# A recurrent attention kernel: ScalarE takes the masked queries and the later key copies from GpSimd, and TensorE multiplies zeros in the prologue

## The chip, the cores and the metric

The kernel runs on one core of a Trainium2 chip. Its time is the device time of that core in microseconds (us). The core has TensorE (PE in the profile), VectorE (DVE), ScalarE (ACT), GpSimd (POOL) and SyncE (SP, which only issues DMAs here). They run at the same time, each in its own program order, and meet at semaphores. A ScalarE function comes from a table; a change of function group (square root, SiLU, sigmoid) puts a table load ahead of the activation.

## The reference

The input x has 4 sequences of 256 tokens with 256 channels. It is normalised (xn), and two branches are joined: x + attention(xn) * silu(experts(xn)).

The attention has 32 heads of 8 channels and goes through each sequence in 16 minibatches of 16 tokens. For each (sequence, head) pair it keeps a weight W1 (8 by 8) and a bias b1, and updates them after every minibatch:

```
Z1 = xk @ W1 + b1
grad = ln_fused_l2_bwd(Z1, xv - xk, ln_w, ln_b)
Z1_bar = xq @ W1 - eta * tril(xq @ xk.T) @ grad + b1 - tril(eta) @ grad
W1 = W1 - (eta_last * xk).T @ grad
b1 = b1 - sum(eta_last * grad)
out = xq + ln(Z1_bar, ln_w, ln_b)
```

The rows are then normalised and multiplied by o_w. The expert branch routes each token to 2 of 8 experts (256 to 2 x 128 to 256).

## The kernel before

**Tiling.** The 1024 tokens lie in 8 tiles (groups) of 128 rows: group j holds 32 tokens of each of the 4 sequences, that is two minibatches of 16. The 128 (sequence, head) pairs are the partitions of the recurrence.

**VectorE** runs the recurrence, one minibatch after another, in `minibatch` (16 calls, n = 0 to 15). A call multiplies keys by token (`KT`) with W (line 821), reduces (832), forms six small products, writes the variances `sxx` (846), and then needs ScalarE's square root (`sv`, semaphore `rstd`) at line 853. It ends with the gradient product (880), its reduction (885) and the new W. Between these steps other work is put as fills. The first minibatch of group j also transposes the keys and targets of group j + 1 out of PSUM (`KP`, `QP`, semaphore `pair_done`); it waits for `kts` before it reads `KT` of its own group.

**GpSimd** has a list written out by hand. For each group j from 1 to 7: `pad_grads(j-1)` (line 374, two halves), four or five `hidden_product(i)` (lines 350 and 355: expert slot i's gate times share, times up), four `mask_scores(j, i)` (line 290), `bias_targets(j+1)` (329 copies the keys from by-channel `KP` to by-token `KT`, 331 adds a bias to the targets), and at the end of the group `masked_queries(j+1)` (339: four multiplications by a head mask, from `xqT` into `xqm`). `masked_queries(0)` and `(1)` stand in the prologue, ahead of `lower_tiles(2, NG)`.

**ScalarE** copies PSUM out (`scores_out`, line 565; `expert_slot`, gate 582 and up 583; `xn_out`, 528) and takes the square roots (`step_std`, 571 and 572). In group j from 2 on its order is: one expert slot, a table load for the square root (`preload_sqrt`, 591), `scores_out(j, 1)`, `step_std(2j+1)`, `scores_out(j, 2)`, slot, `scores_out(j, 3)`, slot, `scores_out(j, 4)`, `preload_sqrt`, `step_std(2j+2)`, and the rest of the group's slots, the first of which loads the SiLU table. `expert_slot(i)` for i = 10, 18, 26 first writes a pair's output (`output_rows`, 587, semaphore `g`).

**TensorE** follows the same plan: `expert_slot(i)` computes slot i's 24 products (1174; it waits until ScalarE has emptied slot i-2) and slot i-2's product with `down` (1187; it waits for GpSimd's `hT`, and where a pair of tiles begins, for `g`); `tile(j, i)` makes a quarter of the scores (1133; it waits for the previous quarter's copy and for `queries`, the masked queries); `group_end(j-1)` multiplies by the padded gradients (1215), `group_start(j)` by W (1201), `next_pair_rows` makes keys and targets for two groups later. The expert slots are spread over groups 1 to 7 as 3, 5, 5, 5, 5, 5, 4.

**The prologue** fills the first 57 us. TensorE first multiplies seven zero matrices (`pe_warm`, line 1074), then makes key rows, rates and target rows of tile 0, transposes tiles 1 to 3 (`xn_channels`, 1081) when ScalarE has normalised them (518), and waits for their copy `xn_out` (528) before the keys of tile 1 (1115). In ScalarE's order `xn_out` of tiles 1 to 3 stands behind `input_std(2, 4, 8)`, the square root that tiles 4 to 7 need (507, released by VectorE).

The new ScalarE steps sit in this loop:

```
for j in range(1, NG):            # ScalarE
    ...
    scores_out(j, 1); step_std(2 * j + 1)
    ...                           # keys_by_token(j + 1) comes here
    scores_out(j, 2)
    ...
    scores_out(j, 4); preload_sqrt(2 * j + 1); step_std(2 * j + 2)
    ...                           # masked_queries(j + 1) comes here
    for i in slots: expert_slot(i)
```

Of the kernel before, what the change touches and what calls it, by code (L numbers as in the profile page):

```python
# [22 lines left out]
P = 128  # L23
B, L, HS = 4, 256, 256
NH, HD, K = 32, 8, 16
NG = 8
# [23 lines left out]
def build(nc, x_bt_d, small_d, wkv_d, wq_d, wlrt_d, gup_d, down_d, wo_d, out_d):  # L50
# [3 lines left out]
    with ExitStack() as ctx:  # L54
# [228 lines left out]
        def _(pool):  # L283
# [41 lines left out]
            def bias_targets(j):  # L325

                pool.wait_ge(S_["pair_done"] if j else S_["pair0T"], j or 1)
                if j:
                    pool.tensor_copy(KT[:, j % 2, :, 0:HD], KP[:, j % 2, 0:HD, :].rearrange("p c t -> p t c")).then_inc(S_["kts"], 1)
                q = QP[:, j % 2, :, :]  # L330
                pool.tensor_tensor(q, q, gb[:, :].unsqueeze(1).broadcast_to([P, GT, HD]), ALU.add).then_inc(S_["targets"], 1)

            def masked_queries(j):

                pool.wait_ge(S_["qchc"], 2 + 2 * (j // 4))
                if j >= 2:
                    pool.wait_ge(S_["sc"], 4 * (j - 1))
                for h in range(4):
                    pool.tensor_scalar(xqm[:, j % 2, :, :, h, :], xqT[:, :, :, GT * j:GT * j + GT],
                                       cmask[:, h:h + 1], 0.0, ALU.mult, ALU.add).then_inc(S_["queries"], 1)  # L340
# [92 lines left out]
            masked_queries(0)  # L433
            masked_queries(1)
# [24 lines left out]
            for j in range(1, NG):  # L459
# [22 lines left out]
                if j + 1 < NG:  # L482
                    masked_queries(j + 1)
# [13 lines left out]
        def _(act):  # L497
# [69 lines left out]

            def step_std(n):
# [20 lines left out]
            def preload_sqrt(n):  # L589

                act.activation(warm[:, n:n + 1], eps[:, :], ACT.Sqrt)  # L591
# [40 lines left out]
            step_std(0)  # L632
            input_std(2, 4, 8)
            xn_out((2, 4), 2, 1, 4)
# [13 lines left out]
            preload_sqrt(1)  # L648
            step_std(2)
# [5 lines left out]
            query_rows(1)  # L655
            for i in range(2, 5):
                scores_out(0, i)
            step_std(3)
            slot = 0
            for j in range(1, NG):  # L660
# [7 lines left out]
                else:  # L668
# [5 lines left out]
                    if j == 6:  # L674
                        norm_z(0)
                    scores_out(j, 2)
# [10 lines left out]
                if j == 4:  # L687
                    scores_out(j, 4)
                for i in slots:
                    expert_slot(i)  # L690
            act.wait_ge(S_["small2"], 16)
# [377 lines left out]
        def _(pe):  # L1069
# [184 lines left out]

            pe.wait_ge(S_["xn0"], 1)
# [7 lines left out]
            rates(0, 1)  # L1263
            pe.wait_ge(S_["wt"], 1)
            target_rows(0, bank[5][:, 0:256]).then_inc(S_["pair0"], 1)
            xn_channels((2, 4), 1, 4)
            pe.wait_ge(S_["xnTc"], 3)
# [59 lines left out]
            def zero_products(count):  # L1327
                for _ in range(count):
                    pe.matmul(bank[1][:, 0:256], pe_warm[:, 0:P], pe_warm[:, :], start=True, stop=True)

# [62 lines left out]
```

## Time and profile before

| what | value |
|---|---|
| median of 3 runs | 233.45 us (232.33 to 238.2) |
| the profiled execution | 233.13 us |
| its span, first to last instruction | 231.2 us |
| TensorE busy | 194.6 us (84%) |
| VectorE busy | 198.5 us (86%) |
| ScalarE busy | 115.7 us (50%) |
| GpSimd busy | 154.4 us (67%) |
| mean granted TensorE clock | 0.938 |

1.93 us of the profiled execution lie outside its span. "Busy" counts the time in which an engine executes; the rest is idle or issue time. Times in the timelines count from the span's start. A matmul in float32 shows as two records. "Granted clock" is 1.0 at the full 2.4 GHz and 0.5 at 1.2 GHz; a value between them is a stretch that has both.

### The profile page before, as it was taken

Reading aid. Unit: us, or ns where it says so; the run is one execution under the profiler, and the core shown is the slowest. Engines: PE = TensorE matmul, PEld = TensorE weight load, DVE = VectorE, ACT = ScalarE, POOL = GpSimd, SP = SyncE. Lnnn points to the kernel's source line nnn. Section 1 sums busy time; section 2 is a strip of 40 time slices with the busy share of each in tenths; the row PEclk is TensorE's granted clock in tenths of the full one; section 3 lists DMA queues with packets and bytes.
Section 4 is the critical chain, followed back from the end, with each engine's and each line's share of the span. In section 5 each row is a group of like instructions: output and inputs, shape, how many; then the busy total and the mean of one; then the engine's idle time right before and its main releaser. Section 6 shows DMA issues by size and latency. Waiting matters only on the chain.

```text
span 231.2 us, 5305 instructions
## 1 busy us (share of the span) xinstructions
PE 194.6 (84%) x1893; PEld 154.4 (67%) x1893; DVE 198.5 (86%) x525; ACT 115.7 (50%) x235; POOL 154.4 (67%) x212
## 2 busy tenths in 40 slices
PE   8533999778789979889999985999799599998772
PEld 6313567256678768677968873879588488866551
DVE  2899999999995999999999999999999999206962
ACT  2462179553529063736555755157564556147230
POOL 2314539897779458597687649769999977464234
PEclk9975899979999979999999999799999799988998
DMA  5995200217613000374120044103000300400022
GB/s 166 374 405 169 75 4 0 71 37 157 204 12 91 3 0 10 91 119 65 27 73 3 0 100 135 48 10 91 0 3 10 93 3 0 145 40 0 3 91 91
DMA packets 26000, 17.44 MB, mean 75 GB/s; under 512 B 10552, under 2 KB 24312, under 8 KB 25464
## 3 DMA queue, kind: packets, MB, share of 16 engines
q1 hardware_dynamic: 25464, 16.25, 25.2%
q10 hardware_dynamic: 512, 0.87, 1.2%
q8 instruction: 15, 0.25, 0.4%
q14 instruction: 9, 0.07, 0.1%
HBM read 15.22 MB, written 1.87 MB: 74 GB/s over the span
## 4 chain that ended last, share of the span: by engine, by line
DVE 38%; PE 34%; ACT 8%; POOL 8%; issue 7%; DMA 2%; POOLq 0%; SPq 0%; DVEq 0%; ACTq 0%
PE bank L1174 9%; PE bank L1215 7%; PE bank L1187 5%; PE bank L1133 5%; DVE pr L821 4%; DVE bank L832 4%; DVE pr L880 4%; DVE dW L885 3%; PE bank L1201 3%; POOL hT L355 2%; POOL gw L350 2%; DMA small<-in_small 2%; POOL sgpad L374 2%; PE bank L1251 2%; PE bank L1109 1%
## 5 line engine op out<-in xcount | busy, mean ns | idle before, releaser
L1174 PE MATMUL bank<-xn_hi,gup_hi 128*128 128x256 f32 x128 | 41.0, 320 | 1.6 <-ACT up L583 1.6
L1187 PE MATMUL bank<-down,hT 128*128 128x256 f32 x128 | 34.4, 393 | 4.5 <-ACT G L587 2.5
L350 POOL TENSOR_TENSOR gw<-gate,share 128x256 f32<-128x256 f32 x32 | 23.4, 730 | 21.5 <-ACT gate L582 21.0
L1174 PE MATMUL bank<-xn_hi,gup_lo 128*128 128x256 f32 x128 | 36.9, 288 | 0.0
L1174 PE MATMUL bank<-xn_lo,gup_hi 128*128 128x256 f32 x128 | 36.9, 288 | 0.0
L290 POOL TENSOR_TENSOR A<-A,mask 128x256 f32<-128x256 f32 x32 | 23.5, 735 | 13.2 <-ACT A L565 13.2
L1174 PEld LDWEIGHTS bank<-xn_hi,gup_hi 128*128 128x128 f32 x128 | 25.1, 196 | 7.6 <-issue 4.2
L1187 PEld LDWEIGHTS bank<-down,hT 128*128 128x128 f32 x128 | 22.9, 198 | 7.1 <-issue 2.7
L565 ACT ACTIVATE A<-bank,one 128x256 f32<-128x256 f32 x32 | 15.0, 469 | 23.2 <-PE bank L1133 23.2
L1174 PEld LDWEIGHTS bank<-xn_hi,gup_lo 128*128 128x128 f32 x128 | 25.2, 197 | 0.2
L355 POOL TENSOR_TENSOR hT<-gw,up 128x256 f32<-128x256 f32 x32 | 23.4, 730 | 2.9 <-PE bank L1187 0.5
L1174 PEld LDWEIGHTS bank<-xn_lo,gup_hi 128*128 128x128 f32 x128 | 25.2, 197 | 0.0
L1215 PE MATMUL bank<-sgpad,A 128*32 128x32 f32 x512 | 20.3, 207 | 5.4 <-POOL sgpad L374 5.4
L582 ACT ACTIVATE gate<-bank 128x256 f32<-128x256 f32 x32 | 12.3, 384 | 25.0 <-PE bank L1174 20.5
L1215 PEld LDWEIGHTS bank<-sgpad,A 128*32 128x32 f32 x512 | 19.5, 124 | 7.7 <-issue 7.7
L1133 PE MATMUL bank<-xqm,xkT 32*32 32x128 f32 x512 | 20.5, 274 | 4.4 <-ACT A L565 2.7
L821 DVE TENSOR_TENSOR pr<-KT,bank 128x1152 f32<-128x1152 f32 x16 | 21.6, 1350 | 0.3
L832 DVE TENSOR_REDUCE bank<-pr 128x128 f32<-128x1152 f32 x16 | 21.4, 1337 | 0.2
L1133 PEld LDWEIGHTS bank<-xqm,xkT 32*32 32x32 f32 x512 | 11.9, 104 | 13.5 <-issue 9.6
L880 DVE TENSOR_TENSOR pr<-KP,bank 128x1152 f32<-128x1152 f32 x15 | 20.3, 1354 | 0.5
L591 ACT ACT_TABLE_LOAD x16 | 20.5, 1283 | 0.3
L885 DVE TENSOR_REDUCE dW<-pr 128x72 f32<-128x1152 f32 x15 | 20.2, 1350 | 0.5
(158 smaller groups left out, 436.7 us busy)
## 6 DMA issues: line engine op xcount, KB each, us to landing
wblk<-w_blocks SPq DMA_DIRECT2D x8, 512.0 KB, 4.0
share<-shares SPq DMA_DIRECT2D x8, 512.0 KB, 8.3
sgpad<-in_gup SPq DMA_DIRECT2D x1, 1024.0 KB, 9.6
G<-in_gup SPq DMA_DIRECT2D x1, 1024.0 KB, 11.7
down<-in_down SPq DMA_DIRECT2D x1, 1024.0 KB, 14.2
xkT<-in_x_bt SPq DMA_DIRECT2D x1, 1024.0 KB, 4.8
out<-G SPq DMA_DIRECT2D x4, 256.0 KB, 2.5
wkv<-in_wkv ACTq DMA_DIRECT2D x1, 512.0 KB, 4.2
```

The costliest lines, as they stand in the source:

```text
L290: pool.tensor_tensor(scores, scores, mask_bc, ALU.mult).then_inc(S_["masked"], 1)
L350: pool.tensor_tensor(gw[:, :], gate[:, i % 2, :], share[:, pair % 2, e, :], ALU.mult).then_inc(S_["gw"], 1)
L355: pool.tensor_tensor(hT[:, i % 2, :], gw[:, :], up[:, i % 2, :], ALU.mult).then_inc(S_["h"], 1)
L591: act.activation(warm[:, n:n + 1], eps[:, :], ACT.Sqrt)
L821: v.tensor_tensor(pr1[:, :].rearrange("p (t d c) -> p t d c", d=HD, t=K), kt.unsqueeze(2).broadcast_to([P, K, HD, C1]), W.rearrange("p (d ...
L832: v.tensor_reduce(x_ps, pr1[:, :].rearrange("p (a c) -> p a c", c=C1), AX.X, ALU.add).then_inc(chain, 1)
L880: v.tensor_tensor(pr2[:, :].rearrange("p (d c t) -> p d c t", c=C1, d=HD), kp.unsqueeze(1).broadcast_to([P, HD, C1, K]), sg.unsqueeze(2).b ...
L885: v.tensor_reduce(dW[:, :], pr2[:, :].rearrange("p (a t) -> p a t", t=K), AX.X, ALU.add).then_inc(S_["sg"], 1)
L1133: ins = pe.matmul(bk[32 * b:32 * b + 32, P * hf:P * hf + P], xkT[32 * q:32 * q + 32, hf, j, GT * b:GT * b + GT], xqm[32 * q:32 * q + 32, j ...
L1174: ins = pe.matmul(bank[4 + i % 2][:, 2 * P * g:2 * P * g + 2 * P], w[:, k, e, NI * g:NI * g + NI].bitcast(F32R), x[:, k, 2 * pair:2 * pair ...
L1187: ins = pe.matmul(bank[7][:, HS * r:HS * r + HS], hT[:, i % 2, P * r:P * r + P], down[:, e, :], start=(e == 0 and r == 0), stop=(e == NE - ...
L1215: ins = pe.matmul(bank[hf][rows_j, 4 * HD * r:4 * HD * r + 4 * HD], A[:, j % 2, q, c:c + GT], sgpad[:, j % 2, h, :, :].rearrange("p b d -> ...
```

## The change

Three edits.

1. `masked_queries` moves from GpSimd to ScalarE: four activations with the mask as per-partition scale in place of four GpSimd multiplications, for all 8 groups. `(0)` stands ahead of `step_std(2)`, `(1)` behind `query_rows(1)`, and `(j+1)` behind `step_std(2j+2)`, ahead of the group's remaining expert slots. The key copy of `bias_targets` stays on GpSimd for groups 1 and 2, and for groups 3 to 7 is a ScalarE copy (`keys_by_token`) behind `step_std(2j+1)` and ahead of `scores_out(j, 2)`.
2. In the prologue ScalarE's `xn_out((2, 4), 2, 1, 4)` goes ahead of `input_std(2, 4, 8)`.
3. TensorE gets 2, 7 and 1 zero products in three places of the prologue.

```diff
             def bias_targets(j):
                 pool.wait_ge(S_["pair_done"] if j else S_["pair0T"], j or 1)
-                if j:
+                if j in (1, 2):
                     pool.tensor_copy(KT[:, j % 2, :, 0:HD], KP[...].rearrange("p c t -> p t c")).then_inc(S_["kts"], 1)
-            def masked_queries(j):                      # GpSimd
-                pool.wait_ge(S_["qchc"], 2 + 2 * (j // 4))
-                if j >= 2:
-                    pool.wait_ge(S_["sc"], 4 * (j - 1))
-                for h in range(4):
-                    pool.tensor_scalar(xqm[:, j % 2, :, :, h, :], xqT[:, :, :, GT * j:GT * j + GT],
-                                       cmask[:, h:h + 1], 0.0, ALU.mult, ALU.add).then_inc(S_["queries"], 1)
...
-            masked_queries(0)
-            masked_queries(1)
             lower_tiles(2, NG)
...
-                if j + 1 < NG:
-                    masked_queries(j + 1)
...
+            def masked_queries(j):                      # ScalarE
+                act.wait_ge(S_["qchc"], 2 + 2 * (j // 4))
+                if j >= 2:
+                    act.wait_ge(S_["sc"], 4 * (j - 1))
+                for h in range(4):
+                    act.activation(xqm[:, j % 2, :, :, h, :], xqT[:, :, :, GT * j:GT * j + GT], ACT.Copy,
+                                   scale=cmask[:, h:h + 1]).then_inc(S_["queries"], 1)
+            def keys_by_token(j):
+                act.wait_ge(S_["pair_done"], j)
+                act.copy(KT[:, j % 2, :, 0:HD], KP[...].rearrange("p c t -> p t c")).then_inc(S_["kts"], 1)
...
             step_std(0)
+            xn_out((2, 4), 2, 1, 4)
             input_std(2, 4, 8)
-            xn_out((2, 4), 2, 1, 4)
...
             preload_sqrt(1)
+            act.wait_ge(S_["small2"], 16)
+            masked_queries(0)
             step_std(2)
...
             query_rows(1)
+            masked_queries(1)
             for i in range(2, 5):
                 scores_out(0, i)
...
+                    if j < NG - 1:
+                        keys_by_token(j + 1)
                     scores_out(j, 2)
...
+                if j < NG - 1:
+                    masked_queries(j + 1)
                 for i in slots:
                     expert_slot(i)
...
             rates(0, 1)                                 # TensorE
+            zero_products(2)
             pe.wait_ge(S_["wt"], 1)
             target_rows(0, bank[5][:, 0:256]).then_inc(S_["pair0"], 1)
+            zero_products(7)
             xn_channels((2, 4), 1, 4)
+            zero_products(1)
```

`zero_products(count)` multiplies `pe_warm` by itself into `bank[1]` count times, 128 by 128 by 256; the function only moves up in the source.

## Rows read from the trace of the kernel before

**Rows 1.** The page: chain of waits by engine, share of the span.

```profile
DVE 38%; PE 34%; ACT 8%; POOL 8%; issue 7%; DMA 2%; POOLq 0%; SPq 0%; DVEq 0%; ACTq 0%
```

**Rows 2.** Waits: who waited for whom: us in total, times, longest.

```profile
ACT sv L571 <- DVE sxx L846: 28.9, 12, 5.7
...
PE bank L1215 <- POOL sgpad L374: 5.4, 5, 1.7
```

**Rows 3.** Timeline of VectorE: start us, us, instruction, [idle before, releaser].

```profile
71.80 0.36 DVE L853 RECIPROCAL bank<-sv 128x32 f32<-128x32 f32 x1 [2.62 <-ACT sv L572]
```

**Rows 4.** Chain of waits, end of group 6: start us, us, what.

```profile
179.27 0.20 DVE sxx L846
...
179.71 0.29 ACT sv L572
...
180.02 0.84 ACT L587
...
181.31 0.60 ACT G L587
...
182.06 2.04 PE bank L1187 x4
```

**Rows 5.** Windows: engine busy us (instructions) in a stretch, TensorE clock, DMA.

```profile
15.30:17.50 2.20, 1.92 (x6) 1.08 (x6) 2.17 (x9) 1.29 (x4) 0.00 (x0) 0.50 1.14 413
...
182.00:186.00 4.00, 3.94 (x17) 3.62 (x17) 3.79 (x13) 0.46 (x2) 2.73 (x5) 0.57 0.14 36
186.00:202.00 16.00, 16.00 (x211) 13.71 (x210) 11.52 (x32) 7.96 (x19) 10.91 (x14) 1.00 0.16 45
```

**Rows 6.** GpSimd, line 339: count, duration ns min/median/max.

```profile
L339 POOL TENSOR_SCALAR xqm<-xqT,small x32: 472/478/483, 45.6 to 182.8; 128x256 f32<-128x256 f32 x32
```

**Rows 7.** GpSimd, line 329, the same view.

```profile
L329 POOL COPY KT<-KP x7: 617/625/650, 27.6 to 170.2; 128x256 f32<-128x256 f32 x7
```

**Rows 8.** Chain of waits, end of group 4.

```profile
137.06 1.22 POOL xqm L339 x3
```

**Rows 9.** ScalarE, line 518, durations.

```profile
L518 ACT ACTIVATE xn<-xn,rstd_in x3: 492/492/493, 14.8 to 15.6; 128x256 f32<-128x256 f32 x3
```

**Rows 10.** Timeline of ScalarE: two runs of activations, one after another.

```profile
14.80 1.29 ACT L518 ACTIVATE xn<-xn,rstd_in 128x256 f32<-128x256 f32 x3
...
220.59 1.51 ACT L622 ACTIVATE xqm<-bank,small 128x128 f32<-128x128 f32 x4 [0.70 <-PE bank L1241]
```

**Rows 11.** Timeline of ScalarE: idle time before some instructions.

```profile
19.79 0.30 ACT L507 ACTIVATE std_in<-mv,eps_in 128x4 f32<-128x4 f32 x1 [2.28 <-DVE mv L720]
...
47.09 0.31 ACT L571 ACTIVATE sv<-sxx,eps 128x16 f32<-128x16 f32 x1 [2.35 <-DVE sxx L846]
...
53.82 0.47 ACT L565 ACTIVATE A<-bank,one 128x256 f32<-128x256 f32 x1 [2.83 <-PE bank L1133]
...
124.22 0.31 ACT L571 ACTIVATE sv<-sxx,eps 128x16 f32<-128x16 f32 x1 [2.15 <-DVE sxx L846]
...
167.98 0.31 ACT L571 ACTIVATE sv<-sxx,eps 128x16 f32<-128x16 f32 x1 [1.01 <-DVE sxx L846]
...
179.50 0.31 ACT L571 ACTIVATE sv<-sxx,eps 128x16 f32<-128x16 f32 x1 [1.36 <-DVE sxx L846]
```

**Rows 12.** Timeline of TensorE: products and idle time before them.

```profile
10.13 1.13 PE L1109 MATMUL bank<-wt,xnT 128*128 128x256 f32 x4 [1.31 <-DVE wt L746]
15.35 1.92 PE L1081 MATMUL bank<-small,xn 128*128 128x128 f32 x6 [4.09 <-ACT xn L518]
...
42.06 3.70 PE L1088 MATMUL bank<-xnT,wq 128*128 128x512 f32 x8 [0.94 <-ACT xkT L535]
...
47.59 0.64 PE L1133 MATMUL bank<-xqm,xkT 32*32 32x128 f32 x16 [1.61 <-POOL xqm L339]
...
95.05 0.39 PE L1174 MATMUL bank<-xn_hi,gup_hi 128*128 128x256 f32 x1 [0.92 <-ACT up L583]
...
182.06 1.19 PE L1187 MATMUL bank<-down,hT 128*128 128x256 f32 x2 [2.48 <-ACT G L587]
```

More of the change, by code:

```diff
@@ L566, in scores_out @@
                                bias=one[:, 0:1]).then_inc(S_["scored"], 1)
+            def masked_queries(j):
[7 more added lines that the diff above has]
+                act.wait_ge(S_["pair_done"], j)
+                act.copy(KT[:, j % 2, :, 0:HD], KP[:, j % 2, 0:HD, :].rearrange("p c t -> p t c")).then_inc(S_["kts"], 1)
             def step_std(n):
@@ L688, in _ @@
                     scores_out(j, 4)
+                if j < NG - 1:
+                    masked_queries(j + 1)
                 for i in slots:
                     expert_slot(i)
-            act.wait_ge(S_["small2"], 16)
             preload_sqrt(0)
@@ L1253, in project, with zero_products @@
                 ins.then_inc(S_["o"], 1)
+            def zero_products(count):
+                for _ in range(count):
+                    pe.matmul(bank[1][:, 0:256], pe_warm[:, 0:P], pe_warm[:, :], start=True, stop=True)
             pe.wait_ge(S_["xn0"], 1)
@@ L1326, in _ @@
                 project(f)
-            def zero_products(count):
-                for _ in range(count):
-                    pe.matmul(bank[1][:, 0:256], pe_warm[:, 0:P], pe_warm[:, :], start=True, stop=True)
             pe.wait_ge(S_["zc"], 8)
```

## The prediction, made before the changed kernel was run

> **What bounds the kernel now.** I read the chain of waits on the page first: VectorE has 38% of it, TensorE 34%, ScalarE and GpSimd 8% each [rows 1]. So no engine bounds it alone, and GpSimd's share is small although it is busy for two thirds of the span. The list of waits says who is early: ScalarE waited 28.9 us in total, 12 times, for VectorE's variances [rows 2]. VectorE thus leads through the loop over groups. The reader should check the other direction, VectorE waiting for ScalarE: the one long such wait is 2.62 us at 71.80, in group 2 [rows 3]. Then comes the question where VectorE's lead passes to the end. The chain at the end of group 6 answers it: VectorE's variances at 179.27, ScalarE's square roots, a SiLU table load at 180.02, the copy of an output pair (line 587) at 181.31, and only then TensorE's product at 182.06 [rows 4], which had been waiting for 2.48 us [rows 12]. From there TensorE has no gap: in the 16 us from 186 to 202 it is busy for 16.00 at full clock [rows 5]. The end is therefore the variances of minibatch 14, plus what ScalarE does until it writes that output pair, plus a TensorE backlog that nothing shortens.
>
> **What leaves GpSimd.** 32 multiplications of 0.478 us [rows 6] and five copies of 0.625 us [rows 7]: about 15 + 3 = 18 us of its time. Is that time on the path? In the end stage GpSimd's masked queries (the last at 182.8 [rows 6]) stand beside TensorE's busy stretch, whose start ScalarE decides [rows 4]. One place has them on the chain, 1.22 us and a fourth instruction at 137.06, in group 4 [rows 8]. What is late next there is VectorE: ScalarE waits for it again by 167.98 (1.01 us) and 179.50 (1.36 us) [rows 11]. I take 0 us for the relief of GpSimd. Its two bounds: nothing, and a gain of the 5.4 us that TensorE spent waiting for GpSimd's padded gradients [rows 2].
>
> **What ScalarE gets.** No row shows a masked query on ScalarE. The nearest is the scaled copy of line 518: same size, same function, scale by a per-partition column, no table load before it. Three take 1.29 us and one lasts 0.492, so one follows another after (1.29 - 0.492) / 2 = 0.40 us [rows 9, 10]. Four cost 1.6 us. The ends: 0.35 us each (line 622, half the size, four in 1.51 us [rows 10]) gives 1.4; 0.492 each, without overlap, gives 2.0. A key copy costs the same 0.4 to 0.5 us.
>
> Place by place:
> - `masked_queries(0)`: ScalarE was idle for 2.35 us before `step_std(2)` at 47.09 [rows 11]; 1.6 us fit. TensorE's first scores, which waited 1.61 us for GpSimd at 47.59 [rows 12], start about 1 us sooner, but their copy stands behind that same `step_std(2)`: 0 us.
> - `masked_queries(1)`: ScalarE was idle for 2.83 us before the second scores copy at 53.82 [rows 11]; 0 us. Without that cover it would be 1.6 us on the path into group 1.
> - `keys_by_token`, five times: behind the square roots, so VectorE does not wait for it there; it delays one scores copy by about 0.45 us. VectorE needs `KT` only in the next group. 0 us, at most 5 x 0.45 = 2.3 us.
> - `masked_queries(2)` to `(6)`: they stand behind `step_std(2j+2)` and ahead of the table load and the gates of the group's last slots. Queued behind them are the gates, then GpSimd's products and padded gradients, then TensorE. At 95.05 TensorE already waited 0.92 us for such a gate [rows 12]; it will wait 1.6 us longer. VectorE does not feel this until ScalarE's next square root comes late, and there ScalarE had 2.15 us to spare at 124.22 [rows 11]: 1.6 us fit. In groups 4 and 5 GpSimd's own 4 x 0.478 = 1.9 us are gone from the same stretch, so ScalarE's 1.6 replace them. 0 us.
> - `masked_queries(7)`: between the square roots of 179.71 and the table load of 180.02 [rows 4]. No cover: TensorE is waiting for what comes behind it, and the backlog behind is solid. **+1.6 us**, whole, on the path. GpSimd's copy of this work, now gone, gives nothing back, since the hidden product after it needs the gate that ScalarE makes late.
>
> **The prologue.** `xn_out` sooner: the copy waited behind a square root that VectorE released at 19.79 [rows 11]; its input is there when the transposes end at 15.35 + 1.92 = 17.3 [rows 12], so the keys of tile 1 come some 2.5 us sooner. The stretch after the 4.09 us wait of TensorE ran at 0.50 of the clock, 1.2 GHz [rows 5, 12]; with zeros in the wait it should stay at 2.4 GHz, and the transposes and key rows are shorter. A zero product is a 128x256 product in float32; two take 1.13 us with their fill at full clock [rows 12], so at most 0.57 us each: two are 1.1 us in a wait of 1.31, seven are 4.0 us in one of 4.09 [rows 12]. If the clock is low they overrun the wait of 4.09 by about 3 us, which `xn_out` hides again, because before it started only after 19.79. What does the head start buy? TensorE next meets ScalarE's copies, which go by VectorE's order (high halves, sigmoid, square roots): at 42.06 it waited 0.94 us for one [rows 12], and now waits more than 2. VectorE has no room to gain in (2.17 us busy of 2.20 [rows 5]). 0 us; bounds -0.5 us (the group 1 chain starts a little warmer) and +1 us (the longer wait ahead of 42.06 costs clock).
>
> **The rule on ports.** The removed GpSimd instructions last 0.472 to 0.483 us and 0.617 to 0.650 us over the whole span [rows 6, 7], beside a VectorE that is nearly always busy: neither engine seems to block the other, and I take 0 us. The Trainium skill, page "SBUF — State Buffer", section "Who interferes with whom", says that VectorE and GpSimd share a port pair, that a VectorE instruction with two SBUF inputs and a GpSimd instruction that reads SBUF block each other, and that ScalarE never waits; by that the move would also make VectorE faster. That mechanism is one form of rival C.
>
> **The sum.** 1.6 us on the path. The profiled execution took 233.13 us, 1.93 us of it outside the span of 231.2; 233.13 + 1.6 = 234.7. The median of the three runs, 233.45, lies 0.3 us above that execution, less than the sum is sure to.
>
> **The rivals.**
> - **B, ScalarE's delay is paid more than once.** The longer waits of TensorE (0.92 + 1.6 = 2.5 us at 95.05) are like the 2.48 us before 182.06, behind which the clock was 0.57 for 4 us [rows 5, 12]: 4 x 0.43 = 1.7 us lost. Then TensorE is 3.3 us late in group 3, 1.2 more than the 2.15 to spare [rows 11], and VectorE stalls: 234.7 + 1.2 = 235.9. In the full form no slack is left and each of the groups 1 to 6 pays its 1.6 us: 233.1 + 9.6 = 242.7, **slower**. It decides from the point where ScalarE reaches a square root after VectorE's variances. For: the spare times of 1.01 and 1.36 us [rows 11] are under 1.6. Against: those two come where GpSimd's load falls away too.
> - **C, VectorE gets ahead.** GpSimd's instructions hold VectorE up unseen, or the stall of 2.62 us [rows 3] goes away. If one of the removed multiplications had blocked VectorE in each of the groups 1 to 6, it would be 6 x 0.48 = 2.9 us earlier: 234.7 - 2.9 = 231.8; the stall gives 234.7 - 2.6 = 232.1. Against: the even durations [rows 6, 7]; and the stall starts at a chain that VectorE's own third minibatch releases, through gates that the change leaves alone.
> - **D, GpSimd was the limit.** TensorE's 5.4 us of waiting for padded gradients [rows 2] go, and they counted: 233.1 - 5.4 = 227.7. Against: ScalarE kept waiting for VectorE [rows 2], so the time returns as that wait.
> - **E, it changes nothing.** Masked queries at the end of group 6 hidden: 233.1. It needs VectorE or the output copy to be earlier by 1.6 us, for which I see no row.
>
> **How the numbers follow.** My case (234.7, its own range 233.4 to 236) has 0.56; B in the small form 0.11 and in the full form 0.07; C 0.13; E 0.08; D 0.05. The range goes from 231.5 to 237.0: it takes in C, E, my case and small B, with 0.3 us either way for the runs, and leaves out D and full B. Two per cent of 233.45 is 4.7 us, about what a measurement of this kernel can tell from no change (its three runs spread over 5.9 us); 228.8 and 238.1 are the bounds. Faster is D: 0.05. Slower is full B: 0.07. The rest, 0.88, is the same.
>
> **What would show it.** TensorE's granted clock near 1.0 from 11 to 25 us, the key rows of tile 1 starting near 18.4, and yet VectorE's variances of minibatch 2 and of 14 at the same times as before (within 0.3 us). ScalarE: four copies in 1.6 us between lines 572 and the SiLU load, the output copy (587) at 182.9 in place of 181.31, and TensorE's product behind it at 183.7. GpSimd 18 us less busy. I am wrong if the variances of minibatch 14 move by more than 1 us (down: C or D; up: B), if TensorE's stretch behind 183.7 has gaps, or if four masked queries take much other than 1.6 us.

## The result and the profile after

The changed kernel took **241.07 us** (median of 4 runs, 237.81 to 242.2); the kernel before took 233.03 us in the same series (232.33 to 238.2). The ratio is 1.0246, with an interval of 1.0179 to 1.0312. A second series, run later as an experiment, gave 239.28 us and 1.0279 [1.0182, 1.0376]. The ratios leave out executions more than 1.5% above the fastest of their kernel, so they are smaller than the ratio of the two medians. The forecast was 234.7 us, with a range up to 237.0: too low. Both series say slower; whether the loss is above or below 2% they leave just open.

The profiled execution is one of the longer ones: 242.2 us, 9.1 us more than the profiled one of before. Its page:

```profile
span 240.4 us, 5346 instructions
...
PE 205.8 (86%) x1913; PEld 161.5 (67%) x1913; DVE 198.3 (82%) x525; ACT 131.0 (55%) x272; POOL 137.2 (57%) x175
...
DVE 52%; PE 28%; ACT 7%; issue 6%; DMA 3%; POOL 2%; POOLq 0%; DVEq 0%; SPq 0%; ACTq 0%
```

GpSimd is 17.2 us less busy, as planned, and ScalarE 15.3 us busier. The chain has shifted from TensorE and GpSimd to VectorE [rows 1]. I take VectorE's sixteen variances as milestones, because ScalarE's root, and through it everything else, hangs on them. `sxx(n)`, in us from the span's start:

| n | 0 | 4 | 5 | 9 | 10 | 14 | 15 | product at the end of group 6 | span |
|---|---|---|---|---|---|---|---|---|---|
| before | 16.69 | 68.44 | 81.01 | 123.91 | 135.09 | 179.19 | 190.91 | 182.06 | 231.2 |
| after | 17.86 | 69.56 | 86.17 | 129.02 | 141.01 | 184.97 | 196.69 | 189.43 | 240.4 |
| later by | 1.17 | 1.12 | 5.16 | 5.11 | 5.92 | 5.78 | 5.78 | 7.37 | 9.2 |

The reader sees five separate losses, and long stretches where nothing changes: 1.2 us before the first minibatch, 4.0 in minibatch 5, 0.8 in minibatch 10, 1.6 behind minibatch 14, and 1.8 in the tail.

**The start, 1.2 us.** VectorE's first work on the small inputs waits for a SyncE transfer. It began at 6.33 before. Timeline of VectorE after:

```profile
7.49 0.17 DVE L741 TENSOR_TENSOR g<-small 128x8 f32<-128x8 f32 x1 [2.04 <-DMA small<-in_small]
```

The same transfer, by the list of DMA issues in the first 9 us, took 4.9 us from issue to landing before and 6.1 us after:

```profile
small<-in_small SPq DMA_DIRECT2D x1, 252.5 KB, 4.9
```

```profile
small<-in_small SPq DMA_DIRECT2D x1, 252.5 KB, 6.1
```

**Minibatch 5, 4.0 us.** The reader should follow the chain of waits of the changed kernel from GpSimd's padded gradients to VectorE's reciprocal:

```profile
62.20 1.06 POOL sgpad L365
...
63.40 2.83 PE bank L1222 x64
66.24 1.05 PE bank L1140 x16
...
67.84 1.07 PE bank L1140 x16
68.91 2.86 PE bank L1181 x12
71.77 1.71 PE bank L1194 x4
73.48 1.05 PE bank L1140 x16
...
75.04 1.28 ACT L592
```

The same chain before, for comparison:

```profile
61.08 1.06 POOL sgpad L374
...
62.27 2.19 PE bank L1215 x64
64.46 0.61 PE bank L1133 x16
...
65.62 0.64 PE bank L1133 x16
66.26 1.63 PE bank L1174 x12
67.89 0.86 PE bank L1187 x4
68.75 0.61 PE bank L1133 x16
...
69.88 1.28 ACT L591
```

Every TensorE piece got longer at an unchanged size (the twelve expert products 2.86 against 1.63 us), and the windows say why: the granted clock is one half, 1.2 GHz.

```profile
64.00:69.00 5.00, 4.41 (x84) 3.42 (x80) 4.93 (x11) 0.49 (x2) 3.13 (x5) 0.55 0.19 36
69.00:74.00 5.00, 5.00 (x28) 4.13 (x32) 1.29 (x6) 1.12 (x3) 1.81 (x3) 0.50 0.40 106
74.00:80.00 6.00, 6.00 (x42) 4.68 (x35) 2.93 (x12) 5.39 (x11) 3.21 (x4) 0.65 0.00 1
```

Before, the clock was 1.00 in all three. What TensorE did ahead of the fall, and what VectorE paid at its end, stand in two timeline rows of after:

```profile
63.40 2.83 PE L1222 MATMUL bank<-sgpad,A 128*32 128x32 f32 x64 [3.27 <-POOL sgpad L365]
```

```profile
76.97 0.36 DVE L860 RECIPROCAL bank<-sv 128x32 f32<-128x32 f32 x1 [6.68 <-ACT sv L573]
```

TensorE waited 3.27 us where it had waited 1.67, and VectorE waited 6.68 us for the root where it had waited 2.62 [rows 3]. The difference of those two, 4.06 us, is the loss. The stall of [rows 3], which I had put under "C" as something that might go away, is where the kernel was exposed.

**The end of group 6, 1.6 us**, in the chain of waits, answering to [rows 4]:

```profile
185.69 0.29 ACT xqm L561
...
186.09 1.29 ACT xqm L561 x3
187.39 1.28 ACT L588
188.69 0.61 ACT G L588
...
189.43 2.05 PE bank L1194 x4
```

This is the predicted step: variances to product took 2.79 us before (182.06 - 179.27) and 4.38 us here (189.43 - 185.05), 1.59 more.

**The tail** is the last projection, at 1.2 GHz in this execution for part of its length: 5.39 us where 3.71 stood. In the second series' profile of the same kernel it took 3.69. Timelines of TensorE, this profile and that one:

```profile
230.82 5.38 PE L1258 MATMUL bank<-wo,xqm 128*128 128x256 f32 x16 [1.59 <-DVE xqm L976]
```

```profile
227.09 3.69 PE L1258 MATMUL bank<-wo,xqm 128*128 128x256 f32 x16 [1.59 <-DVE xqm L976]
```

So it is not a fixed part of the change. Whether the change makes it more frequent is open. Over all 18 profiles of this document the last projection took 3.69 us in nine and 5.38 to 6.16 in nine; all five profiles of kernels without added zero products are among the short ones, and nine of the thirteen with added ones (the ten tiny ones at the end of group 6 among them, below) are the long ones. No run tests it.

### The profile page after: what moved, and what is told of

Same layout as the page of the kernel before. It is cut to its first block, busy times and chain, and to the rows that moved or that the text cites. A ratio compares the mean times of both kernels' runs of the same rounds, so it can differ in the third digit from the quotient of the medians.

```text
span 240.4 us, 5346 instructions
## 1 busy us (share of the span) xinstructions
PE 205.8 (86%) x1913; PEld 161.5 (67%) x1913; DVE 198.3 (82%) x525; ACT 131.0 (55%) x272; POOL 137.2 (57%) x175
## 4 chain that ended last, share of the span: by engine, by line
DVE 52%; PE 28%; ACT 7%; issue 6%; DMA 3%; POOL 2%; POOLq 0%; DVEq 0%; SPq 0%; ACTq 0%
PE bank L1181 9%; DVE bank L839 6%; PE bank L1194 6%; DVE pr L887 6%; DVE pr L828 6%; DVE dW L892 6%; PE bank L1222 4%; PE bank L1140 4%; DMA small<-in_small 3%; PE bank L1258 2%; PE bank L1208 2%; DVE QP L780 1%; ACT xqm L561 1%; DVE bank L882 1%; DVE bank L860 1%
## 5 line engine op out<-in xcount | busy, mean ns | idle before, releaser
L1181 PE MATMUL bank<-xn_hi,gup_hi 128*128 128x256 f32 x128 | 41.9, 327 | 3.6 <-ACT up L584 3.5
L1194 PE MATMUL bank<-down,hT 128*128 128x256 f32 x128 | 36.4, 411 | 6.1 <-ACT G L588 6.1
L1181 PE MATMUL bank<-xn_lo,gup_hi 128*128 128x256 f32 x128 | 37.9, 296 | 0.0
L1181 PE MATMUL bank<-xn_hi,gup_lo 128*128 128x256 f32 x128 | 37.9, 296 | 0.0
L1181 PEld LDWEIGHTS bank<-xn_hi,gup_hi 128*128 128x128 f32 x128 | 26.0, 203 | 9.9 <-issue 5.3
L1194 PEld LDWEIGHTS bank<-down,hT 128*128 128x128 f32 x128 | 24.5, 211 | 8.7 <-issue 6.3
L1181 PEld LDWEIGHTS bank<-xn_lo,gup_hi 128*128 128x128 f32 x128 | 26.2, 205 | 0.0
L1222 PE MATMUL bank<-sgpad,A 128*32 128x32 f32 x512 | 19.1, 202 | 5.5 <-POOL sgpad L365 5.5
L1222 PEld LDWEIGHTS bank<-sgpad,A 128*32 128x32 f32 x512 | 18.2, 118 | 7.8 <-issue 7.8
L1140 PE MATMUL bank<-xqm,xkT 32*32 32x128 f32 x512 | 22.0, 290 | 1.5 <-ACT A L552 1.5
```

What stands on the lines that cost most here:

```text
L1140: ins = pe.matmul(bk[32 * b:32 * b + 32, P * hf:P * hf + P], xkT[32 * q:32 * q + 32, hf, j, GT * b:GT * b + GT], xqm[32 * q:32 * q + 32, j ...
L1181: ins = pe.matmul(bank[4 + i % 2][:, 2 * P * g:2 * P * g + 2 * P], w[:, k, e, NI * g:NI * g + NI].bitcast(F32R), x[:, k, 2 * pair:2 * pair ...
L1194: ins = pe.matmul(bank[7][:, HS * r:HS * r + HS], hT[:, i % 2, P * r:P * r + P], down[:, e, :], start=(e == 0 and r == 0), stop=(e == NE - ...
L1222: ins = pe.matmul(bank[hf][rows_j, 4 * HD * r:4 * HD * r + 4 * HD], A[:, j % 2, q, c:c + GT], sgpad[:, j % 2, h, :, :].rearrange("p b d -> ...
```

## Experiments

Each kernel is the kernel before, or the changed one, with the edit shown. "Step n" is the time from `sxx(n-1)` to `sxx(n)` in the profiled execution.

### Which of the three edits costs

**The prologue alone**: the kernel before with the sooner copies and the ten zeros.

```diff
+            xn_out((2, 4), 2, 1, 4)
             input_std(2, 4, 8)
-            xn_out((2, 4), 2, 1, 4)
...
+            zero_products(2)    # and (7), (1) in their places
```

> Theory P (the prologue is harmless and TensorE's clock falls in group 1 only because of the ScalarE edit): variances of minibatch 4 and 5 as far apart as before (12.6 us), time 233 (within 0.5%). Rival Q (the head start and the zeros let TensorE wait 2.9 us ahead of 43 us, and the lower clock there or the later start carries on): 235 to 238, minibatch 5 over 14 us behind minibatch 4.

Four runs, 233.58 to 239.16, median 237.87; three of the four lie at 237.3 or more, and there is no ratio. The kernel before had a median of 234.37 in that series and itself went up to 238.62, so this points to a loss and does not show one. (The kernel also has the wait for `small2` at its new place.) In the profile the inputs are late (7.22), and steps 5 and 13 are 13.3 and 12.2 against 12.6 and 11.3. Its clock did not fall in group 1: there TensorE stood still for 0.56 us between two of the 64 products with the padded gradients, without a releaser that the profile shows ("issue"). That is most of the 0.75 us of step 5, and it comes back below.

**The ScalarE edit alone**: the changed kernel with the prologue of before.

```diff
-            xn_out((2, 4), 2, 1, 4)
             input_std(2, 4, 8)
+            xn_out((2, 4), 2, 1, 4)
...
-            zero_products(2)    # and (7), (1)
```

> Theory P: nearly all of the loss: 238 to 241, with TensorE at 1.2 GHz from its wait for the padded gradients of group 0 on (62 to 78 us) and VectorE 4 us later from minibatch 5 on, plus 1.6 us at the end of group 6. Rival Q: 234.7, the 1.6 us alone, TensorE at full clock in groups 1 and 2.

237.16 us (234.69 to 239.62), ratio 1.0045 [0.9935, 1.0154]. Inputs at 6.62, step 5 12.6. The wait before the product at the end of group 6 is 6.06 us, and step 10 is 12.0 in place of 11.2: ScalarE reached that root late. Its timeline there:

```profile
124.94 0.47 ACT L552 ACTIVATE A<-bank,one 128x256 f32<-128x256 f32 x1 [0.44 <-PE bank L1140]
125.31 0.30 ACT L572 ACTIVATE sv<-sxx,eps 128x16 f32<-128x16 f32 x1
```

There is no idle before the root, where the kernel before had 2.15 us [rows 11]: the spare time is used up, and 0.8 us goes to VectorE.

**The zeros only**, and **the sooner copies only**. The zero products need nothing else; both kernels also have the wait for `small2` at its new place.

```diff
+            zero_products(2)
             pe.wait_ge(S_["wt"], 1)
             target_rows(0, bank[5][:, 0:256]).then_inc(S_["pair0"], 1)
+            zero_products(7)
             xn_channels((2, 4), 1, 4)
+            zero_products(1)
```

> Only the zero products are added to the kernel before. If the prologue has nothing to give (VectorE has no gap in it): fast runs at 232.5 to 233.5, and what differs comes from where TensorE's clock falls later. If the zeros themselves are the harm (a later start, or the last product in the way of the transposes): VectorE's first variances 0.9 us later or more, 234 or more at the fast end.

```diff
+            xn_out((2, 4), 2, 1, 4)
             input_std(2, 4, 8)
-            xn_out((2, 4), 2, 1, 4)
```

> Only xn_out goes ahead of input_std. If the zeros alone are the prologue's harm: small inputs land at 6.2 to 6.6 us as in the kernels without zeros, fast runs at 232.5 as before. If any head start of TensorE in the prologue brings the fall of the clock in group 1: 238 and a step of 16 us from minibatch 4 to 5.

The zeros alone: 239.75 us (238.84 to 240.67), ratio **1.0264 [1.0175, 1.0354]**, as much as the whole change. The copies alone: 232.98 us over 10 runs, 0.9964 [0.9924, 1.0004]. With the zeros alone, group 1 goes as in the changed kernel; timelines of TensorE and VectorE:

```profile
63.56 3.60 PE L1215 MATMUL bank<-sgpad,A 128*32 128x32 f32 x64 [3.28 <-POOL sgpad L374]
```

```profile
76.78 0.36 DVE L853 RECIPROCAL bank<-sv 128x32 f32<-128x32 f32 x1 [6.33 <-ACT sv L572]
```

Step 5 is 16.3 and step 13 12.2, and inputs came at 7.56. So the loss needs none of ScalarE's new work. The reader should note that group 1 is half of it: of 7.6 us of longer span (238.8 against 231.2), 1.2 are the start, 3.7 step 5, 0.9 step 13 and 2.4 the last projection at the low clock (6.12 against 3.69 us), less 0.8 between minibatch 15 and that projection.

### Is it the wait in group 1

**Four more zeros in that wait**, on top of the zeros-only kernel:

```diff
                 if j == 1:
                     expert_slot(slots.pop(0))
+                    for _ in range(4):
+                        pe.matmul(bank[7][:, 0:256], pe_warm[:, 0:P], pe_warm[:, :], start=True, stop=True)
                 group_end(j - 1)
```

> The prologue's zeros and 4 more in TensorE's wait in group 1. If the loss of the prologue's zeros (6.5 us with them alone) is the later landing of 1 us and the fall of the clock in group 1: minibatch 5 comes 12.6 to 13 us after 4 in place of 16.3, and the time is 235 to 236. If the clock does not matter: 239.5 as with the prologue's zeros alone.

236.3 us (234.67 to 237.63), ratio 1.0141 [1.007, 1.0212]: none of its four runs overlaps the four of the zeros-only kernel, and the medians lie 3.45 us apart. The two ran in different series and on different chips; the kernel before had 233.32 and 233.41 us there, and the intervals of the two ratios overlap. Timeline of TensorE:

```profile
60.30 1.89 PE L1309 MATMUL bank<-pe_warm 128*128 128x256 f32 x8
63.74 2.18 PE L1215 MATMUL bank<-sgpad,A 128*32 128x32 f32 x64 [1.55 <-POOL sgpad L374]
```

The wait is 1.55, the 64 products take 2.18 at full clock, and step 5 is back at 12.6. What remains of the zeros' loss, 1.5 us of span over before (232.7 - 231.2), is the late start: its first variances stand at 18.12, 1.43 after those of before. This profile is also free of the zeros-only kernel's step of 12.2 and of its slow last projection, which stand 80 us and more behind the filled wait. So 3.7 of the 6.1 us between the two profiles lie where the edit is; for the rest the two kernels have one profile each, which is too few.

**Six zeros in the same place of the changed kernel** (as above, `range(6)`).

> Six zero products of 0.43 us fill TensorE's wait of 3.3 us ahead of the products with the padded gradients of group 0. If the loss in group 2 is the clock alone: TensorE stays at 2.4 GHz from 60 to 80 us, minibatch 5 comes 12.6 us after minibatch 4 as before (16.6 in the changed kernel), and the time is 4 us under the changed kernel's, about 236 to 237. If the 4 us come from ScalarE's order or from GpSimd, nothing changes: 241.

237.33 us (236.48 to 242.68), 1.0125 [1.0035, 1.0215]. The median improved on the changed kernel's 241.07 and 239.28, but the profile shows another path: the clock fell earlier, at 48 to 56, TensorE came late and the zeros overran the padded gradients; steps 4 and 5 cost 1.3 and 0.9 more. This run does not show the mechanism cleanly.

### ScalarE's queries at another place

**`masked_queries(7)` ahead of the last scores copy** of group 6, in the changed kernel:

```diff
                 expert_slot(slots.pop(0))
+                if j == NG - 2:
+                    masked_queries(j + 1)
                 if j != 4:
                     scores_out(j, 4)
...
-                if j < NG - 1:
+                if j < NG - 2:
                     masked_queries(j + 1)
```

> The masked queries of group 7 go ahead of the last scores copy of group 6, where ScalarE has 1.4 us or more to spare. If they are paid at the end of group 6: the output copy (line 587 of the kernel before) follows minibatch 14's square roots by 1.6 us in place of 3.2, and the time is 1.6 us under the changed kernel's, some 239.4. Rival: TensorE's backlog or VectorE takes the time back, no gain: 241.

236.34 us (235.72 to 236.79), 1.0093 [1.0021, 1.0165]. Timeline of ScalarE:

```profile
180.64 0.31 ACT L572 ACTIVATE sv<-sxx,eps 128x16 f32<-128x16 f32 x1 [2.71 <-DVE sxx L855]
180.85 0.29 ACT L573 ACTIVATE sv<-sxx,eps 128x16 f32<-128x16 f32 x1
181.16 1.28 ACT L588 ACT_TABLE_LOAD   x1
182.45 0.60 ACT L588 ACTIVATE G<-bank 128x512 f32<-128x512 f32 x1
```

The load follows the root at once, and variances (180.41) to product (183.20) is 2.79 us again, as before: the 1.6 us is this step and nothing else. The rest of the gain came from elsewhere: no fall in group 1, and step 10 at 11.2. TensorE waited 3.27 us at 63.59 here as well, but its clock did not fall, and step 5 is 12.6. The same wait does not always have the same end.

**All of ScalarE's queries sooner, old prologue**: `masked_queries(2)` ahead of `scores_out(1, 2)`, the later ones ahead of `scores_out(j, 4)`.

```diff
+                if 1 < j < NG - 1:
+                    masked_queries(j + 1)
                 if j != 4:
                     scores_out(j, 4)
...
-                if j < NG - 1:
-                    masked_queries(j + 1)
```

> ScalarE makes all masked queries of groups 2 to 7 ahead of a scores copy, not between the square roots and the gates; prologue as before. If the place was the whole cost of the ScalarE edit: 1.6 us at the end of group 6 and 0.8 us at minibatch 10 go, and the time is the kernel before's, 233 (within 0.5%). If relieving GpSimd is worth something once ScalarE's cost is hidden: 230 to 232. If the queries only delay the scores copies instead: 235 as with the ScalarE edit alone.

235.18 us (10 runs, 232.78 to 238.61), 1.0061 [1.0008, 1.0113]. Step 10 is 11.2 again, but step 11 is 11.4 in place of 10.2: in this profile VectorE waits 1.32 us for the root of minibatch 10, so what left one step had come up in the next:

```profile
137.32 0.36 DVE L861 RECIPROCAL bank<-sv 128x32 f32<-128x32 f32 x1 [1.32 <-ACT sv L573]
```

(In the kernel below with the same order of ScalarE and late zeros, both steps are as before.) No gain in the time: GpSimd's relief of 17 us is worth nothing that these ratios can measure.

### The two kernels again

No edit; the kernel before, with ten runs, and the changed one.

> The kernel before, profiled again. If the later start of the kernels with the prologue's edits (SyncE's small inputs landed 0.3 to 1.3 us later in them) is chance: landing between 6.3 and 7.7 us on another execution, too. If it belongs to those kernels: 6.3 to 6.6 again. In both theories VectorE's minibatches keep their steps (12.6 us from 4 to 5, 11.2 from 9 to 10) unless TensorE's clock falls in group 1; then the step from 4 to 5 is longer and the time near the slow end of the runs, 238.

> The changed kernel, profiled again. Theory P (TensorE's waits of 3.3 us in group 1 and 3.5 us ahead of group 2's last products let the clock fall at some executions and not at others): runs spread from 237.5 to 242; a profile without a fall in group 1 shows 12.6 us from minibatch 4 to 5 and a time near 237.5. Rival R (the 4 us are a fixed cost of ScalarE's or GpSimd's order): 16.6 us again with the clock high, and no run under 240.

Before: 233.91 us, 231.46 to 239.59, 0.9985 [0.9926, 1.0043]. In this profile TensorE waited 3.28 us ahead of the padded gradients, the clock fell for 3 us only, and step 5 took 13.7. Changed: 239.28 us (236.79 to 240.79). The profiled one, the fastest, has no fall in group 1, but 11.9 in step 10 and a wait of 6.06 us in group 6. So the loss of 4 us is not a fixed part of the change: it stands in one of the changed kernel's two profiles.

Its step 5 is still 13.5, and this has another source, which the reader finds in the timeline of TensorE:

```profile
65.85 0.22 PE L1222 MATMUL bank<-sgpad,A 128*32 128x32 f32 x1 [0.71 <-issue]
```

The last of the 64 products stands alone, 0.71 us behind the others, and nothing that the profile shows held it. Such a standstill, at 65 to 67 us and in the middle of equal products, is in five of the 18 profiles, 0.36 to 1.04 us long: the prologue alone, this one, the ten tiny products in the prologue, six zeros in group 1, and all queries sooner with late zeros. Their steps 5 are 13.3, 13.5, 14.6, 15.5 and 14.0; in the third and fourth the clock also fell, at 68 us. So step 5 has two ways to get longer, and only one begins with the wait for the padded gradients. What causes the standstill is open.

### Why the inputs land later

In the runs so far the small inputs were late in every kernel with ten or more added zero products, most of which had them in the prologue (the one without, all queries sooner with late zeros, below, had 7.20). One theory was contention (TensorE's early work), the other the size of TensorE's program. **Ten zero products of 8 columns far from the prologue**, at the end of group 6, keep the size and do nothing early; **the same ten at the prologue places** keep the place and nearly no work; **the changed kernel with eight zeros** keeps the work and is smaller.

```diff
+                    if i == 26:                         # expert_slot
+                        pe.wait_ge(S_["pair_done"], 7)
+                        for _ in range(10):
+                            pe.matmul(bank[6][:, 0:8], pe_warm[:, 0:P], pe_warm[:, 0:8], start=True, stop=True)
```

> The kernel before with ten zero products of 8 columns (in place of 256) at the end of group 6: TensorE's program has 1913 products like the changed kernel's, but almost no added work and none in the prologue. Theory S (the later landing of the small inputs belongs to the size of TensorE's program: 6.2 to 6.6 us with up to 1909 products, 6.9 to 7.8 with 1913 or more, in 14 profiles): 6.9 or later, and the time 1 us or more over the kernel before's. Rival W (it belongs to what the zeros do): 6.2 to 6.6, time 233.4.

```diff
+            zero_products(2, 8)    # 8 columns; and (7, 8), (1, 8)
```

> The kernel before with the 2, 7 and 1 zero products in the prologue, but of 8 columns: same instructions and places, no warm TensorE. If the later start alone brings the fall of the clock in group 1: a step of 14 to 16 us from minibatch 4 to 5 and 238 to 240, as with full zeros. If the warm clock in the prologue brings it: the step is 12.6 to 13 and the time 234.5. Landing 6.9 us or later by theory S.

```diff
-            zero_products(7)
+            zero_products(5)
```

> The changed kernel with 2, 5 and 1 zero products, 1909 in all. Theory S: small inputs land at 6.2 to 6.6 us, and the time is 1 us or more under the changed kernel's, 237 to 238.5. Rival W: landing at 6.9 or later, time as the changed kernel's, 240.

| kernel | TensorE products (records) | VectorE starts on the inputs | median us, ratio |
|---|---|---|---|
| before | 1893 | 6.33 | 233.03 |
| changed | 1913 | 7.49 | 241.07 |
| ten tiny ones late | 1913 | 7.11 | 234.81, 1.0008 [0.9946, 1.0069] |
| ten tiny ones in the prologue | 1913 | 7.50 | 235.05, 1.0066 [1.0008, 1.0125] |
| changed, eight zeros | 1909 | 6.10 | 238.46, 1.0159 [1.0009, 1.0309] |

The first two rows' times are of the first series. In the series of the last three the kernel before had 234.51.

Work that runs 180 us later makes the inputs late, and the changed kernel with two zeros fewer has them early. Over all 18 profiles, 1893 to 1909 products gave 6.10 to 6.62 us, and 1913 to 1925 gave 6.88 to 7.76 us. Contention from early work falls. The size of TensorE's program tells the two groups apart in every profile, wherever the products stand; how it does that is not shown. The table shows two more things. A late start with hardly any added work costs 0.2 to 1.5 us by the two ratios, and its absence does not save the changed kernel, which still lost its clock in group 1 (wait 3.28, step 5 14.0). And the ten tiny products stand in the very places of the zeros-only kernel, with the same late inputs, yet 1.0066 [1.0008, 1.0125] stands against 1.0264 [1.0175, 1.0354]: most of the zeros' loss belongs to the work that they do, not to their number or place. The profile of the tiny ones is no clean case of it (a wait of 1.67 us, a standstill of 0.36, a fall of the clock from 68 to 71, step 5 14.6).

### Zeros where waits are, and none in the prologue

Three or six zeros in the wait of group 1 and five or two at the end of group 6, added to the kernel before; and three and eight added to the kernel with all queries sooner.

```diff
+                    for _ in range(3):                  # group 1; 6 in the second kernel
+                        pe.matmul(bank[7][:, 0:256], pe_warm[:, 0:P], pe_warm[:, :], start=True, stop=True)
...
+                        pe.wait_ge(S_["pair_done"], 7)
+                        for _ in range(5):              # slot 26; 2 in the second, 8 in the third
+                            pe.matmul(bank[6][:, 0:256], pe_warm[:, 0:P], pe_warm[:, :], start=True, stop=True)
```

> The kernel before with no prologue edit, 3 zero products ahead of group 0's padded-gradient products and 5 in TensorE's 2.5 us wait at the end of group 6. If zeros are harmful as instructions in the program, wherever they stand: small inputs land at 6.9 us or later. If only those in the prologue are: 6.2 to 6.6. The clock then stays at 2.4 GHz at the two places: no fall in group 1 (the slow runs at 238 to 239 go away) and 1 to 1.7 us less at 182 us: 231 to 232.

> The kernel before with 6 zero products in TensorE's wait of group 1 and 2 at the end of group 6 (1909 products), none in the prologue: the wait of up to 3.3 us is filled. If the fall of the clock there makes the slow executions: step from minibatch 4 to 5 of 12.6 to 13.5 us, no run over 236, median 232 to 233. If the fall comes whatever fills the wait: a spread to 238 or 239 as before.

> ScalarE makes the masked queries at the sooner places, with the late zeros (3 and 8) and no prologue edit. If GpSimd's relief is worth nothing: the same as the kernel before with late zeros, 231 to 232. If it is worth something once the clock does not fall: under 231. If ScalarE's queries still cost at the scores copies: 1 us over it, 232 to 233.

233.48 us (12 runs, 230.25 to 235.61), 0.9942 [0.9895, 0.9989]; 233.01 us (10 runs, 231.09 to 234.02), 0.9969 [0.9911, 1.0028]; 234.34 us (12 runs, 230.92 to 235.65), 0.9938 [0.9888, 0.9988]. None of the 34 runs is above 235.65, while the kernel before goes up to 239.6: the spread is smaller, the fast executions hardly faster. These are the best versions I have, and their ratios are 0.3 to 0.6% below the kernel before, with intervals that end between -1.1% and +0.3%: no gain of 2%. Even this is flattering for two of them: over all their runs the first and the third have medians of 233.48 and 234.34 us, and the kernel before 233.41 in the same series (234.51 in that of the second). Their profiles disagree with the simple story: the first still shows a low clock in group 1 at 64 to 71 and the second at 68 to 72 (steps of 15.3 and 15.5), the second although its zeros left no wait ahead of the padded gradients. Neither has a fall at the end of group 6.

## Why the prediction was wrong, point by point

**The step that failed is the prologue.** I costed it at 0, with bounds of -0.5 and +1. The zeros alone measured 1.0264, some 6 us, in four runs. The working was of the right kind for the prologue itself and stopped there. What it got right, by the windows of after from 11 to 25 us: the granted clock is 1.00 (0.77 and 0.50 before).

```profile
11.00:18.00 7.00, 5.50 (x25) 4.30 (x26) 6.89 (x21) 4.52 (x10) 0.72 (x1) 1.00 1.03 403
18.00:25.00 7.00, 5.93 (x20) 3.24 (x18) 6.57 (x27) 2.20 (x7) 3.42 (x3) 1.00 0.39 115
```

The key rows of tile 1 started at 19.47 instead of 20.89 (18.4 plus the late start), and VectorE gained nothing from it: steps 1 to 4 are 13.0, 17.1, 10.2 and 11.5 in both kernels. Two things were missing.

- **Where the head start ends.** I asked which wait it runs into in the prologue, and found 42.06 (now 2.90 us, "more than 2" was right; the clock did fall behind it, 0.51 from 44 to 46 us, and no VectorE step got longer). I did not ask again in group 1. There VectorE's variances, a table load, a gate and GpSimd fix when the padded gradients come (62.1 to 63.3), and TensorE can only wait. In the profiled execution of before it had run at 1.2 GHz from 49 to 52, came late, and waited 1.67 us. With full clock there it waits 3.3 us: in six profiles out of six where that early fall is missing and nothing fills the wait (after, zeros only, before again, ten tiny ones late, last queries sooner, eight zeros). In four of the six the clock then fell, for 3 to 14 us; in two it did not. Behind it stand 64 small products, three quarters of scores and 16 expert products, all on the path to a root for which VectorE already waited 2.62 us [rows 3]. So no slack covers any of it. How often the head start brings this about is less clear: the early fall is missing in five of the eight profiles with full zeros in the prologue, and in three of the ten others.
- **The late inputs**, 1.0 to 1.4 us. I had nothing in the trace for that, and no bound for what a longer program costs before the first instruction matters. An honest bound would have been the length of the wait for that transfer.

The rule in the Trainium skill, page "TensorE: Matmul & The Clock Gate", section "HAM oscillation — how this bites in real kernels", is that idle gaps between bursts of products bring the low clock back. The trace agrees in kind (with 1.7 us less of wait, 1.55 for 3.28, the fall is gone from step 5), but the same wait of 3.27 us was followed by a fall in one kernel and by none in another, and falls also came behind waits of 1.67 and 1.97 and behind none at all (six zeros in group 1). No run here shows what decides.

**ScalarE's steps held.** Four masked queries took 1.69 us (predicted 1.6, bounds 1.4 and 2.0); the count, median and extremes of one by the view of that line:

```profile
L561 ACT ACTIVATE xqm<-xqT,small x32: 491/494/522, 45.8 to 186.9; 128x256 f32<-128x256 f32 x32
...
L567 ACT COPY KT<-KP x5: 623/627/643, 86.9 to 174.7; 128x256 f32<-128x256 f32 x5
```

The key copy was mis-sized, 0.63 for 0.45 us, and cost nothing. `masked_queries(0)` and `(1)` cost nothing, as said. `masked_queries(7)` cost 1.59 us for a predicted 1.6, and moving it takes exactly that away.

**Rival B in its small form was true as well.** Its price was 1.2 us; it measured 0.8 (step 10, in the ScalarE edit alone and in both profiles of the changed kernel, and gone where the queries go sooner). Its way was as written: TensorE waited 3.5 us for the gate (101.79 in the profile of after), the clock fell, and ScalarE came to root 9 with nothing to spare. I had given it 0.11 and should have added it: its conditions stood in the rows, and I took "1.6 fits into 2.15" although rival B computed 3.3. B's full form, one payment for each group, did not come: in the profile of after, steps 6 to 9 and 11 to 15 are unchanged or shorter (in other kernels with the ScalarE edit one more step paid: 11 above, and 9, 11.6 for 10.1, with eight zeros). My sign for B, variances of minibatch 14 more than 1 us later, did come, 5.78 us, but only 0.8 of it is B; that the full form's 242.7 lies near the measured 241.07 and 242.2 is luck.

C and D fell as gains in the time. One place speaks for a part of D, and I had overlooked it: in three of the ten profiles with GpSimd's queries (the prologue alone, zeros only, zeros late) step 13 is 12.2 us. There TensorE waits about 1.65 and 1.02 us for GpSimd between 141 and 150 us, then runs at 1.2 GHz for 6 to 7 us, and VectorE waits 1.0 us for the root of minibatch 12. The second wait in the zeros-only kernel:

```profile
149.36 3.60 PE L1215 MATMUL bank<-sgpad,A 128*32 128x32 f32 x64 [1.02 <-POOL sgpad L374]
```

In this kernel GpSimd's masked queries are on that chain, as at 137.06 in the kernel before [rows 8]. In all eight profiles with the queries on ScalarE step 13 is 11.1. So the relief may spare 1 us in some executions; no experiment isolates this.

Two sums of the prediction were loose. Seven zeros at 1.2 GHz, by its own 0.57 us at full clock, overrun the wait of 4.09 by 3.9 us and not by 3, and 0.3 us above small B ends at 236.2 and not at 237.0. Neither changes the outcome.

**The sum as measured**, on the profiled execution: 1.2 (start) + 4.0 (group 1) + 0.8 (B) + 1.6 (group 6) + 1.8 (tail) = 9.4, less 0.2 that steps elsewhere gave back: 9.2. The first four by themselves would give 240.7. Only the 1.6 was in the forecast. The parts do not add up over medians, though: 1.0264 for the zeros and 1.0045 for ScalarE's work against 1.0246 and 1.0279 for both, because each part moves where the clock falls.

**Open**: why a longer TensorE program makes the first transfers land later (it was seen to set in between 1909 and 1913 products, and no view shows what moves then); why one execution loses the clock behind a wait of 3.3 us and another keeps it; and whether warm zeros in the prologue bring that fall more often through the late start together with the wait, since either alone gave executions with it and without it. Open too are the standstill of TensorE at 65 to 67 us and the slow last projection. With ten to twelve runs of each this could be counted; I have four of the zeros-only kernel.

## What to carry to other kernels

- Follow a head start past the place where it is first hidden, to every later wait of that engine on something that did not move. A wait that grows is not free if the work behind it is on the path: look at the clock behind it and at who is already waiting there.
- Added zero products are work, program length and a shift of the clock's ups and downs. Filling the one wait whose successor is on the path gave time back in one kernel and did not keep the clock up in two others, so count the runs and look at several executions; one profile is one sample.
- Put a moved step into an engine's idle time ahead of the event it waits for, not between that event and the next table load: `masked_queries(7)` cost 1.6 us behind the root and 0 ahead of it.

## What the runs showed of the hardware that was not expected

- The clock can stay low through solid work. From 69 to 74 us TensorE was busy for 5.00 of 5.00 us, and the granted clock was 0.50; the stretch at 1.2 GHz lasted from 64 to 78 us.
- TensorE programs of 1913 products and more had their first inputs 0.3 to 1.7 us later than those of 1909 and fewer, with identical DMA instructions.
- TensorE can stand still among equal products with no wait that the profile shows: 0.36 to 1.04 us, at 65 to 67 us, in five of 18 profiles.
- The same last projection of eight products took 3.69 us in nine profiles and 5.38 to 6.16 in nine, behind waits of 1.3 to 1.6 us for VectorE.
- One kernel on one core spread over 8 us (231.46 to 239.59 in ten runs of the kernel before). Eight to eleven zero products at places of waits, in groups 1 and 6, cut this to 3 to 5 us and hardly moved the fast end.
- A table load followed the square root directly and took 1.28 us, and the activation behind it started 1.29 us after the load did (181.16 and 182.45).
